# Leaving the last, empty edge tile ungathered, and adding the records of neighbouring chunks in pairs, in a relational graph attention kernel

## What is computed

```python
Q = einsum('nc,rch->rnh', x, Wq) + bq     # K and V likewise: R x N x HEADS x OUT
q_i, k_j, v_j = Q[edge_type, dst], K[edge_type, src], V[edge_type, src]
score = sum(q_i * k_j, axis=-1) * scale
seg = dst * R + edge_type
alpha = softmax of score over the edges of one seg
out = segment_sum(v_j * alpha, dst, N) + bias
y = layernorm(x + out)
```

## Time and profile before

| | |
|---|---|
| runs | 2515.57 us median of 3 (2513.05 to 2515.9) |
| the profiled execution | 2516.02 us, span 2514.2 us |
| busy share | DVE 68%, POOL 65%, PE 64%, ACT 47% |
| chain that ended last, by engine | POOL 33%, PE 26%, issue 16%, DVE 12%, ACT 7%, DMA 5% |
| its largest lines | L405 22%, L566 21%, L410 11%, L800 6% |
| POOL's indirect DMAs | L405 x832, 951 ns each; L410 x432, 952 ns; L386 x400, 953 ns |
| adds of the records | L1154 x52, 158 ns each |
| granted clock of TensorE, mean | 0.736 of 2.4 GHz |

### The profile page before, as it was taken

One profiled execution on the slowest core, in us unless ns is written; L12 is line 12 of the kernel. 1 busy time (PEld: TensorE's weight loads), 2 busy tenths in 40 slices (PEclk: granted clock), 3 DMA queues, 4 the chain that ended last, 5 costly groups with the idle time before them and its releaser, 6 DMA issues.

```text
span 2514.2 us, 26371 instructions
## 1 busy us (share of the span) xinstructions
PE 1600.0 (64%) x5873; PEld 1108.5 (44%) x5873; DVE 1718.9 (68%) x3712; ACT 1192.3 (47%) x4083; POOL 1628.7 (65%) x1745
## 2 busy tenths in 40 slices
PE   6999999999991354555555555555555455545546
PEld 2444544444440344444444444444444444444434
DVE  8888454443434777777777777777777777777758
ACT  2223111000001566666666666666666666666654
POOL 1000667777777777777777777777777777777504
PEclk9999999999995566665566566665665666666667
DMA  6333889999999766666666666666666666666406
GB/s 199 113 117 122 303 297 345 363 362 364 362 363 317 237 203 203 203 203 203 201 203 203 203 201 203 203 203 205 200 205 203 202 203 203 203 204 201 135 1 188
DMA packets 289040, 556.32 MB, mean 221 GB/s; under 512 B 44077, under 2 KB 171135, under 8 KB 288882
## 3 DMA queue, kind: packets, MB, share of 16 engines
q0 software_dynamic: 106496, 327.26, 43.1%
q1 hardware_dynamic: 146148, 159.43, 19.0%
q10 hardware_dynamic: 36238, 67.94, 7.6%
HBM read 399.62 MB, written 154.83 MB: 221 GB/s over the span
## 4 chain that ended last, share of the span: by engine, by line
POOL 33%; PE 26%; issue 16%; DVE 12%; ACT 7%; DMA 5%; SPq 1%; DVEq 0%; ACTq 0%; POOLq 0%
POOL region L405 22%; PE sums L566 21%; POOL region L410 11%; ACT region L800 6%; DVE region L881 5%; DMA region<-q_tab,qidx 3%; PE sums L627 2%; DVE region L1026 1%; DVE pairs L1024 1%; ACT pairs L789 1%; DVE acc L1087 1%; DVE region L1165 1%; PE sums L563 1%; DVE region L1168 1%; PE bank L587 0%
## 5 line engine op out<-in xcount | busy, mean ns | idle before, releaser
L627 PE MATMUL sums<-region 128*128 128x130 f32 x3328 | 775.0, 416 | 765.5 <-ACT region L800 745.7
L627 PEld LDWEIGHTS sums<-region 128*128 128x128 f32 x3328 | 704.9, 317 | 823.2 <-ACT region L800 818.1
L405 POOL DMA_INDIRECT region<-kv_tab,kvidx x832 | 790.9, 951 | 257.9 <-issue 245.0
L800 ACT ACTIVATE region<-region 128x64 f32<-128x64 f32 x3328 | 821.5, 333 | 0.0
L566 PE MATMUL sums<-region,acc 128*128 128x512 f32 (+2 forms) x1568 | 674.5, 577 | 1.0 <-DVE region L1003 0.8
L386 POOL DMA_INDIRECT region<-q_tab,qidx x400 | 381.1, 953 | 376.0 <-DMA q_tab<-region 253.2
L789 ACT COPY pairs<-region 128x1024 f32<-128x1024 f32 x208 | 211.2, 1015 | 696.4 <-DMA region<-q_pre 385.6
L1087 DVE TENSOR_TENSOR acc<-acc,sums 128x256 f32 x832 | 348.7, 419 | 271.1 <-PE sums L627 196.3
L410 POOL DMA_INDIRECT region<-q_tab,qidx x432 | 411.4, 952 | 131.6 <-issue 130.1
L566 PEld LDWEIGHTS sums<-region,acc 128*128 128x128 f32 (+1 forms) x1568 | 285.8, 190 | 302.2 <-issue 290.9
L1003 DVE TENSOR_TENSOR region<-sums,region 128x512 f32<-128x512 f32 (+1 forms) x245 | 168.9, 691 | 249.4 <-PE sums L566 249.1
(11 more groups left out here) (188 smaller groups left out, 813.2 us busy)
## 6 DMA issues: line engine op xcount, KB each, us to landing
kv_tab<-region ACTq DMA_DIRECT2D x48, 1280.0 KB, 7.5
q_pre<-region SPq DMA_DIRECT2D x400, 128.0 KB, 5.2
region<-q_pre SPq DMA_DIRECT2D x400, 128.0 KB, 3.5
q_tab<-region SPq DMA_DIRECT2D x48, 640.0 KB, 3.2
region<-q_tab,qidx POOLq DMA_INDIRECT x832, 3.8
region<-kv_tab,kvidx POOLq DMA_INDIRECT x832, 3.6
region<-in_x SPq DMA_DIRECT2D x96, 128.0 KB, 3.2
out<-region SPq DMA_DIRECT2D x48, 128.0 KB, 2.5
```

The costliest lines, as they stand in the source:

```text
L405: pool.indirect_dma_start(ring[:, s % KS, i, :], None, kv_tab, bass.IndirectOffsetOnAxis(ap=kvidx[:, t:t + 1], axis=0)).then_inc(s_got[s % ...
L627: done = nc.tensor.matmul(bank[i][:, h * W:(h + 1) * W], ring[:, q % KS, i, h * P:(h + 1) * P], oneh[:, q % 2, i, :], start=True, stop=True)
L800: done = nc.scalar.activation(ring[:, q % KS, i, h * D:(h + 1) * D], ring[:, q % KS, i, C + h * D:C + (h + 1) * D], ACT.Copy, scale=alT[:, ...
```

## The change

Tile 831 is no longer gathered, neither its kv rows nor its query rows, and `gathered` counts two DMAs less for the last superblock. Its ring slot keeps what it held; its slots take part in nothing, since their one-hot rows are empty.

The tail record of chunk j and the head record of chunk j + 1 are added by one operation on two neighbouring columns of acc, the tail's node and the one after it. `same`, worked out in step 7, is 1 where tail and next head belong to the same node. Then the head's values are added to the tail's column, otherwise they go to the second column, since by the dummies the next head's node is then the one after the tail's. The last tail and the first head remain single. The limit on the addresses falls by one, so that two columns fit.

```diff
--- before.py
+++ after.py
@@ -46,6 +46,8 @@
     G = 32
     NCK = -(-(E + P * NT) // (P * G))
     TT = NCK * G
+
+    USED = -(-(E + P * NT) // P)
     SB = 4
     NSB = TT // SB
     PERC = G // SB
@@ -60,6 +62,7 @@
     AHEAD = [SB if s < 12 else (2, 2, 1, 2, 2)[s % 5] for s in range(NSB)]
     PRE = [s * SB + i for s in range(NSB) for i in range(AHEAD[s])]
     NPRE = len(PRE)
+    assert TT - SB < USED and max(PRE) < TT - SB + AHEAD[NSB - 1] <= USED
     EASE = 72
 
     kv_tab = nc.dram_tensor("kv_tab", (R * N, 2 * C), f32).ap()
@@ -137,6 +140,7 @@
         qidx = sb("qidx", [P, TT], i32)
         n0i = sb("n0i", [1, TT], i32)
         reci = sb("reci", [1, 2 * NCK], i32)
+        same = sb("same", [P, NCK - 1])
         nrel = sb("nrel", [P, TT])
         XF = sb("XF", [P, NCK, P + 1], bf16)
         PEN = sb("PEN", [P, P + 1], bf16)
@@ -228,6 +232,7 @@
         eq, pn = cut(64), cut(64)
         mk = cut(H * 64).rearrange("p (h n) -> p h n", h=H)
         recV = cut(C)
+        pairV = cut(2 * 2 * 32).rearrange("p (h k c) -> p h k c", h=2, k=2)
         stats = cut(2 * 6).rearrange("p (s n) -> p s n", s=2)
         mv = cut(8 * 2).rearrange("p (s n) -> p s n", s=8)
         std, rstd, shift = cut(8), cut(8), cut(8)
@@ -310,7 +315,8 @@
 
         def gathered(s):
 
-            return 16 * sum(2 * SB - n for n in AHEAD[s % KS:s + 1:KS])
+            last = 2 * (TT - USED) if s == NSB - 1 else 0
+            return 16 * (sum(2 * SB - n for n in AHEAD[s % KS:s + 1:KS]) - last)
 
         def piece(s):
 
@@ -402,6 +408,8 @@
                     pool.wait_ge(s_lift, s - QS + 1)
                 for i in range(SB):
                     t = s * SB + i
+                    if t >= USED:
+                        continue
                     pool.indirect_dma_start(ring[:, s % KS, i, :], None, kv_tab,
                                             bass.IndirectOffsetOnAxis(ap=kvidx[:, t:t + 1], axis=0)
                                             ).then_inc(s_got[s % KS], 16)
@@ -664,7 +672,7 @@
             done.then_inc(s_r10, 1)
 
 
-            pe.wait_ge(s_racc, 2 * NCK)
+            pe.wait_ge(s_racc, NCK + 1)
             for t in range(NT):
                 n = nodes(t)
                 if t >= 4:
@@ -934,7 +942,10 @@
                                                         op1=ALU.subtract))
                     both = bank[7][:, 0:4 * NCK].rearrange("p (u c) -> p u c", u=4)
                     c.go(nc.vector.tensor_scalar(reci.rearrange("p (s c) -> p s c", s=2), both[0:1, 2:4, :],
-                                                 float(ACCW - 1), None, ALU.min))
+                                                 float(ACCW - 2), None, ALU.min))
+                    c(nc.vector.tensor_copy(same[:], both[:, 3, 0:NCK - 1]))
+
+                    c.go(nc.vector.tensor_tensor(same[:], same[:], both[:, 2, 1:NCK], ALU.is_equal))
                     nc.vector.tensor_copy(recS[:, :, 0:NCK], both[:, 0:2, :]).then_inc(s_castc, 1)
                     dve.wait_ge(s_castc, 1)
                     c.join()
@@ -1142,18 +1153,36 @@
                                     wn4[0:64, :].unsqueeze(2).broadcast_to([64, H, D]), ALU.mult).then_inc(s_r9, 1)
 
 
+
             dve.wait_ge(s_r10, 1)
-            for j in range(0, 2 * NCK, 4):
+            rv = bank[6][:, 0:P].rearrange("p (h s c) -> p h s c", h=2, s=2)
+            heads, tails = rv[:, :, 0, 1:NCK], rv[:, :, 1, 0:NCK - 1]
+            once = same[:].unsqueeze(1).broadcast_to([P, 2, NCK - 1])
+            c(nc.vector.tensor_tensor(pairV[:, :, 0, 0:NCK - 1], heads, once, ALU.mult))
+            c.go(nc.vector.tensor_tensor(pairV[:, :, 1, 0:NCK - 1], heads, pairV[:, :, 0, 0:NCK - 1], ALU.subtract))
+            c(nc.vector.tensor_tensor(pairV[:, :, 0, 0:NCK - 1], tails, pairV[:, :, 0, 0:NCK - 1], ALU.add))
+
+            def add_record(j, at, width, values):
+                if j > 0:
+                    dve.wait_ge(s_racc, j)
+                nc.vector.tensor_tensor(acc[:, :, bass.ds(at, width)], acc[:, :, bass.ds(at, width)], values, ALU.add
+                                        ).then_inc(s_racc, 1)
+
+            for lo in range(NCK, 2 * NCK, 4):
+                n = min(4, 2 * NCK - lo)
                 _, at = nc.values_load_multi_w_load_instructions(
-                    reci[0:1, j:j + 4], engines=[DVE], min_val=0, max_val=ACCW - 1,
+                    reci[0:1, lo:lo + n], engines=[DVE], min_val=0, max_val=ACCW - 2,
                     skip_runtime_bounds_check_because="the program limits them")
-                for i in range(4):
-                    col = (j + i) // NCK * 32 + (j + i) % NCK
-                    if j + i > 0:
-                        dve.wait_ge(s_racc, j + i)
-                    nc.vector.tensor_tensor(acc[:, :, bass.ds(at[i], 1)], acc[:, :, bass.ds(at[i], 1)],
-                                            bank[6][:, 0:P].rearrange("p (h r) -> p h r", h=2)[:, :, col:col + 1], ALU.add
-                                            ).then_inc(s_racc, 1)
+                for i in range(n):
+                    j = lo - NCK + i
+                    if j < NCK - 1:
+                        add_record(j, at[i], 2, pairV[:, :, :, j])
+                    else:
+                        add_record(j, at[i], 1, rv[:, :, 1, j:j + 1])
+            _, at = nc.values_load_multi_w_load_instructions(
+                reci[0:1, 0:2], engines=[DVE], min_val=0, max_val=ACCW - 2,
+                skip_runtime_bounds_check_because="the program limits them")
+            add_record(NCK, at[0], 1, rv[:, :, 0, 0:1])
 
             def moments(t):
                 n = nodes(t)
```

## The result

| | before | changed |
|---|---|---|
| median of 6 runs | 2515.74 us | 2506.89 us |
| lowest and highest | 2513.05, 2517.26 | 2504.83, 2508.91 |
| profiled execution, span | 2516.02, 2514.2 | 2508.65, 2506.8 |

The ratio is 0.9971 (95% interval 0.9960 to 0.9981), a gain of 4.8 to 10.1 us; its lower end falls just short of the 5.0 us of the 0.2% line. (The recorded ratio isn't the quotient of the two medians, which is 0.9965 and lies inside the interval.) The forecast was 2505.5. The number is near, but the traces show that it is near for a partly wrong reason: the largest term is half missing.

What follows compares the result with a forecast made beforehand. The prediction took the end of the gathers, ACT's drain and DVE's record adds as the path; −2.65 − 8.35 + 0.7 + 0.2 = −10.1 us gave 2505.9 profiled, 2505.5 us median, range 2502.0 to 2510.0.

Steps and rivals of the forecast that it cites:

- Two gathers less: End of the gathers: POOL's last issue and its landing come earlier, −2.65 us, bounds −1.2 and −3.2.
- The records: Edge-record adds on DVE before the last stage: 27 adds and 8 loads take 9.59 instead of 17.94 us, −8.35 us.
- the stall: A 0.40 us stall in the second record add of before; kept in the forecast, with ±0.4 us left for it.
- the load of addresses is dearer than its row says: Rival at the record adds: address loads cost more than the 0.22 us priced, giving 2503.6 us; chance 3%.
- Three operations: DVE makes the pairs ahead of the record adds in three operations, +0.7 us, bounds 0.4 and 1.1.
- Two operations in step 7: Copy and comparison ahead of the copy into recS start PE 0.34 us later; taken as +0.2 us, between 0 and 0.4.
- The last stage keeps its pace: Last stage unchanged since DVE bounds there at either clock; 1 us allowed if PE came out just short.
- The sum: −2.65 − 8.35 + 0.7 + 0.2 = −10.1 us for the whole kernel, 2505.9 profiled and 2505.5 as median.
- The likeliest case: The forecast case for the whole time, 76%, said to reach by itself from 2503.5 to 2508.5 us.
- The clock rose in the drain: Rival: the clock rises one superblock later in the drain (1.3 us lost) or never (+7.4 us, 2512.9); together 8%.
- Hidden gathers: Rival: something other than the last gather's landing releases the drain, so only the records pay, 2508.2 us; chance 6%.
- Moved tiles: Rival: `same` shifts the tiles behind it, making HBM stores dearer; at 4%, +6.5 us, time 2522.1; chance 2%.

Runs made afterwards that it cites:

- the shifted kernel: The kernel before with only reci, the address table, moved by two words (8 bytes); median 2526.37 us against 2518.29, ratio 1.0032.
- the gathers alone: The kernel before with only tile 831's gathers left out, records as before; 2516.66 us against 2518.29, ratio 0.9994.
- the probe: The kernel before with four copies of the addresses, 0 to 3 words off, and record loads of various places and lengths; run once, 2516.09 us.

## Why the prediction was right or wrong, point by point

**Two gathers less, −2.65 us.** Right in its mechanism: the copy came 2.55 us earlier against the issue of the same gather, 3.60 us behind it. DVE did start late, as I had reckoned: its product began 1.41 us after the end of ACT's copy (2362.18 against 2360.77), where before it was 0.09. But the scores ended at 2364.66, and PE took them at 2366.57, so 1.9 us covered it; that matmul stands 6.82 us behind the copy in both traces. To the scalings it is 2.16 us in the two traces and 2.1 in the means (40.1 to 38.1). The 0.4 us lost behind the copy may be the clock or chance; that stays open.

**The records, −8.35 us.** This is the step that failed, by its load term. The adds behaved: 0.29 to 0.30 us apart also at four elements, 166 ns instead of 158. But I priced the 8 loads at 0.22 each, the row of loads that begin at a multiple of 16 bytes, where the new ones begin 8 bytes past one. Those cost 0.63 us more, six times, and the two short ones 0.2 more each: 4.2 us. Aligning them took 4.5 us off PE's wait, 0.3 to 0.4 of it by the stall that was gone, for which I had left ±0.4. The term should have been −4.15, and the wait of PE, with the three operations ahead, fell by 3.5 instead of 7.65. The rival in my text, "the load of addresses is dearer than its row says", had the sign wrong: I took a dearer load for more gain, since there are fewer, and never asked whether the loads that stay are the same loads. The Trainium skill states a floor of about 600 ns for `tensor_load`, without naming the memory ("DMA: Bandwidth & Descriptors", the table on latency and other measured facts). The traces don't agree: four aligned words take 0.34 us.

**Three operations, +0.7.** From 2429.90 to 2430.48, 0.6. Right.

**Two operations in step 7, +0.2.** PE's wait grew by 0.31, as worked out. From there to the first kv gather it is 437.3 us before and 437.7 in the change, while kernels alike in this step differ by over 1 us (437.4 in the shifted kernel, 438.7 with the gathers alone). Whether the 0.3 us arrive at the end can't be told.

**The last stage keeps its pace.** 61.65 and 61.91. Right in the number, but I misread the row behind it: from 2490 to 2495, at the lower clock, PE was busy 4.90 of 5 us and DVE 4.62, which doesn't show that DVE bounds there.

**The sum.** The local spans give 2.1 + 3.25 less 0 to 0.3, about 5.2 us, half of the 10.1 forecast. Both measurements contain it: 4.8 to 10.1 and, the change again, 3.3 to 8.0 us. The first set's median, 8.85 us lower, lies 3.7 us beyond it, and its ratio's 7.3 us lie 2.1 beyond. In the profiled pair the excess is the 2.25 us by which POOL came earlier to tile 830's q gather: the first kv gather came 2.3 us later than before (773.10 against 770.78), and the main loop, from there to tile 828's kv gather, was 4.6 us shorter. That length is 1579.9 to 1582.6 us in the traces that gather all tiles and 1578.1 to 1587.8 in those that don't, with no order in it, so the shorter loop of this pair looks like scatter. That all of the excess is scatter is not shown: with the records' part of the change in the kernel, the ratio gave 0.6 to 2.5 us more than the local spans in all five comparisons, each time within its interval, and in the two without it (the shifted kernel and the gathers alone) it gave none more; no run shows why. So the forecast's 2505.5 was hit by luck, with a term 4.2 us too large and 2 to 4 us of gain that no term of it explains. When the change ran again, it was 5.0 us below the kernel before by the medians and 5.8 by the ratio; the slow end of my range, 2510.0, stands for 5.6 us less than before.

**The likeliest case's lower end.** It was added up wrongly: −0.55 for the gathers, −0.4 for the stall and −0.3 for the joins lead from 2505.5 to 2504.25, with step 7 at nothing to 2504.05, and not to 2503.5. The range began some 0.6 us too low.

**The other rivals.** The clock rose in the drain no later than before: 16 matmuls took 2.03 us from 2402.32 on, when the stretch had begun at 2389.76, so 12.6 us into it, against 13.3 before (2407.42, 2394.17). Hidden gathers are out, by the copy's wait. Moved tiles did not cost the 6.5 us of my rival, but that they cost nothing isn't shown. The first kv gather of the main loop, behind the stages that write the tables, came at 769.6 to 772.9 us in the five traces without `same` (mean 770.9) and at 771.5 to 773.2 in the five with it (mean 772.5). The two groups overlap, and 0.3 us of the difference is the wait at step 7; no run moved the tiles and did nothing else.

## What to carry to other kernels

A price read from a row holds for an instruction with the same operands, and the address is one of them, as the 0.34 and 0.96 us of one load show: before pricing an instruction that stays, look where it now begins. Tables of register values are best laid out so that each load fetches four words from a multiple of 16 bytes, with padding between the parts. And where a change is worth some us of 2500, single medians may mislead by as much; local spans, over several kernels that are alike in that place, tell its parts apart. They should add up to the medians' difference, and what is left over is to be named as open.

## What the runs showed of the hardware

A load of registers from on-chip memory by DVE's sequencer costs 0.34 us for four words from a multiple of 16 bytes, 0.96 us for four words from any other place, and 0.52 to 0.54 for two from either; in the gap between two adds the probe's loads fit about 0.1 us and 0.22 for each access. Put between other work of DVE in the drain, eight loads of 0.34 us did not lengthen it.
